# Spectral weights loaded by two DMA queues, one for each half of the partitions, the two starting at different output channels

## The chip, the cores and the metric

The kernel runs on one core of one Trainium2 chip. The metric is the device time of one execution in microseconds (us). Before the change it is 3788.58 us, the median of 3 runs (3782.95 to 3789.09).

## What is computed

The input x has 16 images of 64 channels of 128 x 128, all float32. It is normalized in 32 groups of two channels, goes through one layer, and is added to the layer's result:

```
x1 = spectral_conv2d(x, w1, w2)        # 16x16 low modes of rfft2, two blocks of rows
x2 = einsum('bchw,oc->bohw', x, conv_w) + conv_b
y  = kan_linear(kan_linear(x1 + x2, k1...), k2...)
return x + gelu(y)

def spectral_conv2d(x, w1, w2):
    x_ft = rfft2(x)
    out_ft[:, :, :16, :16]  = einsum('bixy,ioxy->boxy', x_ft[:, :, :16, :16],  w1)
    out_ft[:, :, -16:, :16] = einsum('bixy,ioxy->boxy', x_ft[:, :, -16:, :16], w2)
    return irfft2(out_ft)
```

The weights w1 and w2 are complex; each comes as a real and an imaginary tensor [input channel i, output channel o, x, y] of 64 x 64 x 16 x 16 float32. These four tensors (w1_r, w1_i, w2_r, w2_i), 4.19 MB each, are what the change is about.

## The kernel before

The program is a row of blocks. At the end of a block all engines wait for each other.

1. `forward` (lines 243 to 476) transforms the 16 images to their low modes and gathers statistics. SyncE (SP) loads each image in 8 DMAs (line 307) of 128 partitions x 8 channels x 128 values; one piece of memory that such a DMA copies is 512 bytes, and there are 1024 of them. The last thing that SP does there is `load_mix_weights(sp, t, weights[:, 2], 0, 0)` (line 343), the load of w1_r.
2. `statistics_and_mix` (lines 479 to 678) turns the statistics into one factor for each channel and image (`VectorE`, DVE, lines 615 to 664, with small matmuls at lines 547 to 558), and multiplies the modes by the weights (`mix_ps`, line 574). SP loads a small table (`pick`, line 539) and then w1_i, w2_r and w2_i (line 541).
3. `inverse_rows` (lines 681 to 785) transforms the result back along the image's height, through DRAM.
4. `second_half` (lines 788 to 1084) does the rest, tile by tile: convolution, the two spline layers, gelu. GpSimd (POOL) has its only work here, one DMA of a tile (line 906) that adds x to the result: 128 partitions x 4 KB, so 128 pieces of 4 KB.

The mix (lines 562 to 579) has two groups g: g = 0 uses w1, g = 1 uses w2. Before a group TensorE (PE) waits until both parts (real and imaginary) of its weights have landed (line 565). A group has 8 steps x; a step is 64 matmuls. A step waits for `normed` (the modes times the factors, which DVE makes at line 675) and for `mix_kept`, which says that ScalarE (ACT) has copied the result of the step but one before out of the PSUM buffer (line 595). ACT stores each copy with two DMAs on its own queue (line 600), and copies into one of two buffers only when the stores of that buffer have landed (line 594).

In SBUF the weights stand with 64 input channels on partitions 0 to 63 for one half of the rows x (8 of 16), and the same 64 input channels on partitions 64 to 127 for the other half. Each weight tensor so takes 8 DMAs of 512 KB (line 147): 4 ranges of 16 output channels, and for each both halves, one after the other. One DMA covers 64 partitions x 16 output channels x 128 values: again 1024 pieces of 512 bytes. All go through the SP queue:

```
    for o0 in range(0, C, MIX_O):
        for half in range(2):
            ...
            sp.dma_start(dst[half * C:(half + 1) * C, o0:o0 + MIX_O, :, :], ...
```

C is 64, MIX_O is 16, SH is 8.

Of the kernel before, what the change touches and what calls it, by code (L numbers as in the profile page):

```python
# [13 lines left out]
B, C, H, W = 16, 64, 128, 128  # L14
# [25 lines left out]
SH = MODES // 2  # L40
PLACES = SH + 1

MIX_O = 16
# [76 lines left out]
def first_half(nc, t):  # L120

    with ExitStack() as ctx:
        def sb(name, shape):
            return ctx.enter_context(nc.sbuf_tensor(name, shape, F32))

        modes = sb("modes", [P, PLACES, 2, 2 * MODES, B])
        stats = sb("stats", [P, B, G, 6])

        big = sb("big", [P, 4, C * W])

        rs_own = sb("rs_own", [P, 2, B])
        rs_neg = sb("rs_neg", [P, 2, B])
        mix_loaded = [[ctx.enter_context(nc.semaphore(f"mix_loaded{g}{part}")) for part in range(2)] for g in range(2)]
        t = dict(t, modes=modes, stats=stats, big=big, rs_own=rs_own, rs_neg=rs_neg, mix_loaded=mix_loaded)
        forward(nc, t)
        statistics_and_mix(nc, t)


def load_mix_weights(sp, t, dst, g, part):

    src = ((t["w1_r"], t["w1_i"]), (t["w2_r"], t["w2_i"]))[g][part]
    for o0 in range(0, C, MIX_O):
        for half in range(2):
            x0 = SH * (half if g == 0 else 1 - half)
            sp.dma_start(dst[half * C:(half + 1) * C, o0:o0 + MIX_O, :, :],
                         src[:, o0:o0 + MIX_O, x0:x0 + SH, :]).then_inc(t["mix_loaded"][g][part], 16)


def place(j):
# [91 lines left out]
def forward(nc, t):  # L243
# [8 lines left out]
    with ExitStack() as ctx:  # L252
# [8 lines left out]
        weights = big[:].rearrange("p i (o x k) -> p i o x k", x=SH, k=MODES)  # L261
# [35 lines left out]
        block = ctx.enter_context(nc.Block())  # L297

        def chunk(k):
            return slice(k * CH_GRP, (k + 1) * CH_GRP)  # L300

        @block.sync
        def _(sp):
            def load(par, b, k):
                src = t["x"][b].rearrange("c h w -> h c w") if isinstance(b, int) else \
                    t["x"][bass.ds(b, 1)].rearrange("a c h w -> h (a c) w")
                sp.dma_start(img[:, par, chunk(k), :], src[:, chunk(k), :]).then_inc(img_loaded[par][k], 16)

            sp.dma_start(dft_h_sb[:], t["dft_h"]).then_inc(tables_loaded, 16)
            load(0, 0, 0)  # L310
            sp.dma_start(eye[:], t["ident"]).then_inc(tables_loaded, 16)
            sp.dma_start(dft_w_sb[:], t["dft_w"]).then_inc(tables_loaded, 16)
            for l, (b_, s_, c_) in enumerate(((t["k1_base"], t["k1_spline"], t["k1_scaler"]),
                                              (t["k2_base"], t["k2_spline"], t["k2_scaler"]))):
                own = slice(l * C, (l + 1) * C)
                sp.dma_start(kan["spline"][own], s_).then_inc(natural_loaded, 16)
                sp.dma_start(kan["scaler"][own], c_).then_inc(natural_loaded, 16)
                sp.dma_start(kan["mats"][own, F_SILU, :], b_).then_inc(natural_loaded, 16)
                sp.dma_start(kan["mats"][own, NF, :], t["conv_w"]).then_inc(natural_loaded, 16)
            for k in range(1, N_GRP):  # L320
                load(0, 0, k)
            for k in range(N_GRP):
                load(1, 1, k)
            for d in range(2):
                sp.dma_start(t["conv_bias"][d * C:(d + 1) * C, :],
                             t["conv_b"].rearrange("(c a) -> c a", a=1)).then_inc(consts_loaded, 16)
            sp.dma_start(t["inv_w_sb"][:], t["inv_w"]).then_inc(consts_loaded, 16)
            sp.wait_ge(mats_ready, 1)
            for l in range(2):
                for d in range(2):  # L330
                    sp.dma_start(t["kan_b"][l][d * C:(d + 1) * C, :],
                                 kan["bias"][l * C:(l + 1) * C]).then_inc(consts_loaded, 16)
            with sp.Fori(1, B // 2) as b2:
                for par in range(2):
                    for k in range(N_GRP):

                        sp.wait_ge(along_h_done, 2 * N_GRP * b2 + (N_GRP * (par - 2) + k + 1))
                        sp.sem_inc(seen_by_sp, 1)
                        sp.wait_ge(stats_ready, 2 * N_GRP * b2 + (N_GRP * (par - 2) + k + 1))
                        sp.sem_inc(seen_by_sp, 1)  # L340
                        load(par, 2 * b2 + par, k)
            sp.wait_ge(consts_loaded, 112)
            load_mix_weights(sp, t, weights[:, 2], 0, 0)

        @block.vector
        def _(dve):
# [132 lines left out]
def statistics_and_mix(nc, t):  # L479
# [13 lines left out]
    with ExitStack() as ctx:  # L493
# [31 lines left out]
        mix_w = [[parts[:, 2], parts[:, 3]], [parts[:, 0], parts[:, 1]]]  # L525
# [9 lines left out]
        block = ctx.enter_context(nc.Block())  # L535

        @block.sync
        def _(sp):
            sp.dma_start(pick_sb[:], t["pick"]).then_inc(pick_loaded, 16)
            for g, part in ((0, 1), (1, 0), (1, 1)):  # L540
                load_mix_weights(sp, t, mix_w[g][part], g, part)

        @block.tensor
        def _(pe):
            pe.wait_ge(set_up, 2)
            for eo in range(2):
                ins = nc.tensor.matmul(ps_mean[:], avg[:], stats[:, :, :, 3 * eo + 1], start=(eo == 0), stop=(eo == 1))
            ins.then_inc(mean_done, 1)
            pe.wait_ge(dev_ready, 1)
            for eo in range(2):  # L550
                nc.tensor.matmul(ps_var[:], avg_sq[:], stats[:, :, :, 3 * eo + 2], start=(eo == 0), stop=False)
            for eo in range(2):
                ins = nc.tensor.matmul(ps_var[:], avg_sq[:], dev_sq[:, eo], start=False, stop=(eo == 1))
            ins.then_inc(var_done, 1)
            pe.wait_ge(rm_ready, 1)
            for i in range(2):
                rows = slice(i * C, (i + 1) * C)
                ins = nc.tensor.matmul(ps_bias[i][rows, :], conv_two[rows], pair_rm[rows, :], start=True, stop=True,
                                       tile_position=(i * C, i * C))
            ins.then_inc(bias_done, 1)  # L560

            pe.sem_inc(mix_done, 2)
            for g in range(2):
                for part in range(2):
                    pe.wait_ge(t["mix_loaded"][g][part], 32 * (C // MIX_O))
                for x in range(SH):
                    u = x % 2
                    pe.wait_ge(normed_ready, SH * g + x + 1)
                    pe.wait_ge(mix_kept, SH * g + x + 1)
                    for at in range(MIX_Q):  # L570
                        for part in range(2):
                            for col in range(2):
                                ky = col * MIX_Q + at
                                ins = nc.tensor.matmul(
                                    ps[u][col * C:(col + 1) * C, at * C:(at + 1) * C],
                                    normed[u][:, ky, 1 - part:3 - part, :, :].rearrange("p f h b -> p (f h b)"), mix_w[g][part][:, :, x, ky],
                                    start=(part == 0), stop=(part == 1), skip_group_check=True,
                                    tile_position=(0, col * C))
                    ins.then_inc(mix_done, 1)
# [534 lines left out]
```

## Time and profile before

| what | value |
|---|---|
| median of 3 runs | 3788.58 us |
| the profiled execution's own time | 3786.73 us |
| its span in the profile | 3784.9 us |
| TensorE busy | 3662.3 us (97% of the span) |
| GpSimd busy | 110.9 us (3%) |
| mix: first matmul to last store issued | 288.95 to 366.7 us of the span |

The profile was taken in one execution, and its times count from the start of the span. PE, DVE, ACT, POOL and SP are the engines; an SPq row is an instruction that SP's queue issues, and its length is the time that issuing took, not the transfer. "DMA share" is the mean busy share of the 16 DMA engines; since the packets of an engine overlap a little, it goes over 1. Lines are those of the kernel before.

### The profile page before, as it was taken

The numbers are of one execution on the slowest core, as the hardware profiler recorded it, in microseconds if no ns is written. First come the engines' busy times: TensorE is split into PE (matmuls) and PEld (weight loads), VectorE is DVE, ScalarE is ACT, GpSimd is POOL, SyncE is SP. The second block draws the span as 40 slices with busy tenths as digits, with TensorE's granted clock in tenths as the row PEclk, the third lists the DMA queues.
The fourth block names the chain that finished last, engine by engine and source line by source line (L and its number), as shares of the span: only waits on it lengthen the run. The fifth ranks groups of instructions, "written<-read, shape, count | busy, mean of one in ns | idle before, by whom it ended". The sixth has DMA issues, their size and how long they took to land.

```text
span 3784.9 us, 101254 instructions
## 1 busy us (share of the span) xinstructions
PE 3662.3 (97%) x37164; PEld 2765.6 (73%) x37164; DVE 3518.6 (93%) x3900; ACT 3391.7 (90%) x3509; POOL 110.9 (3%) x132
## 2 busy tenths in 40 slices
PE   8986599999999999999999999999999999999998
PEld 4446257777777777777777777777777777777774
DVE  7762399999999999999999999999999999999996
ACT  4531399999999999999999999999999999999996
POOL 0000000000000000000000000000000000000000
PEclk9998799999999999999999999999999999999999
DMA  9997622322322322322332332332332232232232
GB/s 263 290 248 152 232 56 60 72 66 60 72 66 60 72 67 60 72 67 60 72 69 57 72 72 55 71 72 56 70 72 57 69 72 58 68 72 58 68 72 45
DMA packets 322041, 328.62 MB, mean 87 GB/s; under 512 B 86864, under 2 KB 251216, under 8 KB 319952
## 3 DMA queue, kind: packets, MB, share of 16 engines
q1 hardware_dynamic: 301008, 256.73, 25.0%
q0 software_dynamic: 18432, 67.12, 11.2%
q10 hardware_dynamic: 2560, 4.20, 0.5%
q8 instruction: 30, 0.49, 0.1%
q14 instruction: 11, 0.09, 0.0%
HBM read 239.88 MB, written 88.08 MB: 87 GB/s over the span
## 4 chain that ended last, share of the span: by engine, by line
PE 87%; DVE 0%; issue 0%; ACT 0%; POOL 0%; POOLq 0%; ACTq 0%; DVEq 0%
PE l_ps L1057 82%; PE y_ps L1044 3%; PE y_ps L1036 2%; DVE cube2l L933 0%; DVE cube3r L933 0%; ACT above L972 0%; ACT size L983 0%; ACT offset L987 0%; ACT S L976 0%; ACT below L980 0%; DVE cube1r L933 0%; DVE cube1l L933 0%; DVE cube0l L933 0%; ACT L976 0%; DVE cube0r L933 0%
## 5 line engine op out<-in xcount | busy, mean ns | idle before, releaser
L987 ACT ACTIVATE offset<-size 128x1024 f32<-128x1024 f32 x1280 | 1240.5, 1044 | 8.1
L933 DVE SCALAR_TENSOR_TENSOR cube0r<-below,offset 128x1024 f32<-128x1024 f32 x256 | 314.3, 1228 | 57.3 <-ACT offset L987 56.7
L1057 PE MATMUL l_ps<-S,turned_w 64*64 64x512 f32 x2048 | 330.5, 592 | 8.1 <-issue 8.1
L1057 PE MATMUL l_ps<-cube1l,turned_w 64*64 64x512 f32 x2048 | 330.0, 589 | 1.0 <-issue 1.0
L1057 PE MATMUL l_ps<-cube0r,turned_w 64*64 64x512 f32 x2048 | 329.9, 591 | 0.6 <-DVE cube0r L933 0.6
L1057 PE MATMUL l_ps<-cube3r,turned_w 64*64 64x512 f32 x2048 | 329.7, 589 | 0.8 <-DVE cube3r L933 0.8
L1057 PE MATMUL l_ps<-below,turned_w 64*64 64x512 f32 x2048 | 329.9, 591 | 0.0
L1057 PE MATMUL l_ps<-cube4r,turned_w 64*64 64x512 f32 x2048 | 329.7, 589 | 0.1
L1057 PE MATMUL l_ps<-cube4l,turned_w 64*64 64x512 f32 x2048 | 329.7, 589 | 0.1
L1057 PE MATMUL l_ps<-cube3l,turned_w 64*64 64x512 f32 x2048 | 329.7, 589 | 0.1
L1057 PE MATMUL l_ps<-cube2r,turned_w 64*64 64x512 f32 x2048 | 329.6, 589 | 0.0
L1057 PE MATMUL l_ps<-cube2l,turned_w 64*64 64x512 f32 x2048 | 329.6, 589 | 0.0
L1057 PE MATMUL l_ps<-bowl,turned_w 64*64 64x512 f32 x2048 | 329.6, 589 | 0.0
L1057 PE MATMUL l_ps<-inner_cube,turned_w 64*64 64x512 f32 x2048 | 329.6, 589 | 0.0
L1057 PE MATMUL l_ps<-cube1r,turned_w 64*64 64x512 f32 x2048 | 329.2, 589 | 0.0
L1057 PE MATMUL l_ps<-cube0l,turned_w 64*64 64x512 f32 x2048 | 329.1, 590 | 0.0
L933 DVE SCALAR_TENSOR_TENSOR cube4l<-above,offset 128x1024 f32<-128x1024 f32 x256 | 314.4, 1228 | 0.0
L942 DVE SCALAR_TENSOR_TENSOR inner_cube<-below,square 128x1024 f32<-128x1024 f32 x256 | 314.4, 1228 | 0.0
L933 DVE SCALAR_TENSOR_TENSOR cube4r<-below,offset 128x1024 f32<-128x1024 f32 x256 | 314.3, 1228 | 0.0
L933 DVE SCALAR_TENSOR_TENSOR cube3l<-above,offset 128x1024 f32<-128x1024 f32 x256 | 314.2, 1227 | 0.0
L933 DVE SCALAR_TENSOR_TENSOR cube3r<-below,offset 128x1024 f32<-128x1024 f32 x256 | 314.1, 1227 | 0.0
L933 DVE SCALAR_TENSOR_TENSOR cube2l<-above,offset 128x1024 f32<-128x1024 f32 x256 | 313.9, 1226 | 0.0
(121 smaller groups left out, 7481.4 us busy)
## 6 DMA issues: line engine op xcount, KB each, us to landing
big<-in_x_dram SPq DMA_DIRECT2D x128, 512.0 KB, 7.0
x_ring<-in_x_dram SPq DMA_DIRECT2D x256, 256.0 KB, 4.0
act_out<-in_x_dram POOLq DMA_DIRECT2D x128, 512.0 KB, 6.8
out_dram<-act_out SPq DMA_DIRECT2D x128, 512.0 KB, 2.7
rows_scratch<-rows SPq DMA_DIRECT2D x16, 1024.0 KB, 7.0
rows_t<-rows_scratch SPq DMA_DIRECT2D x512, 32.0 KB, 5.5
big<-in_spec_w_r_dram SPq DMA_DIRECT2D x16, 512.0 KB, 11.1
big<-in_spec_w_i_dram SPq DMA_DIRECT2D x16, 512.0 KB, 11.2
```

What stands on the lines that cost most here:

```text
L933: nc.vector.scalar_tensor_tensor(out=cube[q][side][:], in0=distance[layer][:], scalar=EDGE - KNOTS[q], in1=offset[layer][q][:], op0=ALU.mi ...
L942: nc.vector.scalar_tensor_tensor(out=inner_cube[:], in0=below[layer][:], scalar=EDGE, in1=square[layer][:], op0=ALU.subtract, op1=ALU.mult ...
L987: nc.scalar.activation(offset[layer][q][:], size[layer][:], ACT.Square, bias=-KNOTS[q]).then_inc(offset_ready[layer], 1)
L1036: nc.tensor.matmul(y_ps[image, n * MM:(n + 1) * MM], conv_t[par][half, image], src[half, i * MM:(i + 1) * MM], start=True, stop=False, ski ...
L1044: ins = nc.tensor.matmul(y_ps[image, at:at + W], rows[half, par, h, :], inv_w_sb[half, i, :], start=False, stop=(h == HH - 1), skip_group_ ...
L1057: ins = nc.tensor.matmul(dst[cols, r * MM:(r + 1) * MM], kan_w[layer][rows_, f, :], src[rows_, n * MM:(n + 1) * MM], start=(f == 0), stop= ...
```

## The change

`load_mix_weights` gets an engine and a half as arguments, and issues the 4 DMAs of that half alone. Half 0 takes the output channels from 0, 16, 32, 48; half 1 takes them from 32, 48, 0, 16. For w1_r, still inside `forward`, SP issues half 0 and then half 1. For w1_i, w2_r and w2_i SP issues half 0 and GpSimd half 1, each from the start of the block of statistics and mix. There is one semaphore for each half, group and part, where there was one for each group and part; TensorE waits for both halves.

```
-def load_mix_weights(sp, t, dst, g, part):
+def load_mix_weights(eng, t, dst, g, part, half):
...
     src = ((t["w1_r"], t["w1_i"]), (t["w2_r"], t["w2_i"]))[g][part]
-    for o0 in range(0, C, MIX_O):
-        for half in range(2):
-            x0 = SH * (half if g == 0 else 1 - half)
-            sp.dma_start(dst[half * C:(half + 1) * C, o0:o0 + MIX_O, :, :],
-                         src[:, o0:o0 + MIX_O, x0:x0 + SH, :]).then_inc(t["mix_loaded"][g][part], 16)
+    x0 = SH * (half if g == 0 else 1 - half)
+    for n in range(0, C, MIX_O):
+        o0 = (n + half * (C // 2)) % C
+        eng.dma_start(dst[half * C:(half + 1) * C, o0:o0 + MIX_O, :, :],
+                      src[:, o0:o0 + MIX_O, x0:x0 + SH, :]).then_inc(t["mix_loaded"][half][g][part], 16)
...
             sp.wait_ge(consts_loaded, 112)
-            load_mix_weights(sp, t, weights[:, 2], 0, 0)
+            for half in range(2):
+                load_mix_weights(sp, t, weights[:, 2], 0, 0, half)
...
             for g, part in ((0, 1), (1, 0), (1, 1)):
-                load_mix_weights(sp, t, mix_w[g][part], g, part)
+                load_mix_weights(sp, t, mix_w[g][part], g, part, 0)
+
+        @block.gpsimd
+        def _(pool):
+            for g, part in ((0, 1), (1, 0), (1, 1)):
+                load_mix_weights(pool, t, mix_w[g][part], g, part, 1)
...
-                    pe.wait_ge(t["mix_loaded"][g][part], 32 * (C // MIX_O))
+                    for half in range(2):
+                        pe.wait_ge(t["mix_loaded"][half][g][part], 16 * (C // MIX_O))
```

What SP issues from the end of `forward` to the start of `inverse_rows`, before (`big` holds the weights):

```order
L147 DMA big<-in_spec_w1_r_dram 64x16x128 x8
L252 UNCONDITIONAL_BRANCH
L537 UNCONDITIONAL_BRANCH
L539 DMA pick_sb<-pick_dram 128x32
L147 DMA big<-in_spec_w1_i_dram 64x16x128 x8
L147 DMA big<-in_spec_w2_r_dram 64x16x128 x8
L147 DMA big<-in_spec_w2_i_dram 64x16x128 x8
```

The same place of SP now (the lines of the changed file are one or two higher):

```order
L148 DMA big<-in_spec_w1_r_dram 64x16x128 x8
L253 UNCONDITIONAL_BRANCH
L539 UNCONDITIONAL_BRANCH
L541 DMA pick_sb<-pick_dram 128x32
L148 DMA big<-in_spec_w1_i_dram 64x16x128 x4
L148 DMA big<-in_spec_w2_r_dram 64x16x128 x4
L148 DMA big<-in_spec_w2_i_dram 64x16x128 x4
```

SP keeps all 8 DMAs of w1_r and half of the DMAs of each of the other three tensors.

GpSimd from its start to its DMA of the second half, before:

```order
L1101 MEMSET const-uint8-127 128x1
L901 UNCONDITIONAL_BRANCH
L903 UNCONDITIONAL_BRANCH
L903 ISA
L906 REGISTER_ALU x4
L906 ISA
L906 DMA act_out<-in_x_dram 128x1024
```

And now:

```order
L1109 MEMSET const-uint8-127 128x1
L545 UNCONDITIONAL_BRANCH
L148 DMA big<-in_spec_w1_i_dram 64x16x128 x4
L148 DMA big<-in_spec_w2_r_dram 64x16x128 x4
L148 DMA big<-in_spec_w2_i_dram 64x16x128 x4
L495 UNCONDITIONAL_BRANCH
L909 UNCONDITIONAL_BRANCH
L911 UNCONDITIONAL_BRANCH
L911 ISA
L914 REGISTER_ALU x4
L914 ISA
L914 DMA act_out<-in_x_dram 128x1024
```

The twelve DMAs that SP lost stand on GpSimd, ahead of everything that it did before, and behind the end of `forward`, since the block begins there.

## Rows read from the trace of the kernel before

**Rows 1.** The page: the span in 40 slices of 94.6 us, PE, DMA

```profile
PE   8986599999999999999999999999999999999998
DMA  9997622322322322322332332332332232232232
```

**Rows 2.** Waits of PE, 259 to 370 us: total, times, longest

```profile
PE mix_ps L574 <- DMA big<-in_spec_w_i_dram: 26.2, 2, 16.0
...
PE mix_ps L574 <- ACT mixed L595: 1.6, 1, 1.6
```

**Rows 3.** Timeline of PE, 268 to 376 us: start, length, what, [idle before]

```profile
288.95 21.98 PE L574 MATMUL mix_ps<-big,stats 128*64 128x64 f32 x384 [10.13 <-DMA big<-in_spec_w_i_dram]
312.48 7.36 PE L574 MATMUL mix_ps<-big,stats 128*64 128x64 f32 x128 [1.55 <-ACT mixed L595]
335.87 28.84 PE L574 MATMUL mix_ps<-big,stats 128*64 128x64 f32 x512 [16.03 <-DMA big<-in_spec_w_i_dram]
375.25 1.23 PE L763 MATMUL rows_ps<-spec,inv_h_sb 64*128 64x512 f32 x2 [10.53 <-DMA spec<-modes_scratch]
```

**Rows 4.** Timeline 268 to 450 us: DVE's chain of statistics, its last steps

```profile
268.02 0.68 DVE L629 TENSOR_TENSOR picked<-mean_bg,pick_sb 128x512 f32<-128x512 f32 x1
...
274.41 0.69 DVE L629 TENSOR_TENSOR picked<-ps_var,pick_sb 128x512 f32<-128x512 f32 x1 [4.98 <-PE ps_var L553]
...
280.75 0.69 DVE L675 TENSOR_TENSOR stats<-modes,rs_neg 128x512 f32<-128x512 f32 x1 [0.35 <-DVE modes L664]
281.36 1.29 DVE L675 TENSOR_TENSOR stats<-modes,rs_own 128x512 f32<-128x512 f32 x2
```

**Rows 5.** Timeline of ACT, 288 to 376 us

```profile
302.54 0.60 ACT L595 ACTIVATE mixed<-mix_ps 128x512 f32<-128x512 f32 x1 [5.57 <-DMA modes_scratch<-mixed]
...
321.09 0.60 ACT L595 ACTIVATE mixed<-mix_ps 128x512 f32<-128x512 f32 x1 [5.73 <-DMA modes_scratch<-mixed]
...
324.94 0.60 ACT L595 ACTIVATE mixed<-mix_ps 128x512 f32<-128x512 f32 x1 [3.25 <-DMA modes_scratch<-mixed]
```

**Rows 6.** Stretches: length, PE, PEld, DVE, ACT, POOL busy, PEclk, DMA share, GB/s

```profile
60.00:230.00 170.00, 170.00 (x1523) 82.14 (x1520) 132.59 (x391) 88.65 (x183) 0.00 (x0) 1.00 1.16 290
263.00:288.00 25.00, 7.46 (x14) 2.53 (x12) 13.71 (x33) 0.22 (x1) 0.00 (x0) 0.57 1.22 194
300.00:321.00 21.00, 18.21 (x320) 17.50 (x315) 10.46 (x17) 2.39 (x4) 0.00 (x0) 1.00 1.17 233
342.00:362.00 20.00, 20.00 (x364) 20.00 (x361) 9.48 (x15) 3.60 (x6) 0.00 (x0) 1.00 0.36 78
```

**Rows 7.** DMAs of w1_r issued 247 to 258 us

```profile
L147 SPq DMA_DIRECT2D big<-in_spec_w_r_dram x5: 2502/2622/3114, 245.3 to 255.8; - x5
...
DMA to landing us min/median/max: 11.0/11.2/11.4
```

**Rows 8.** Timeline of the SP queue, 226 to 262 us (issuing only)

```profile
239.25 19.67 SPq L147 DMA_DIRECT2D big<-in_spec_w_r_dram  x8
259.56 1.99 SPq L539 DMA_DIRECT2D pick_sb<-pick_dram  x1
261.60 0.60 SPq L147 DMA_DIRECT2D big<-in_spec_w_i_dram  x1
```

**Rows 9.** ACT's stores issued 288 to 300 us, beside the weights

```profile
L600 ACTq DMA_DIRECT2D modes_scratch<-mixed x4: 489/494/595, 293.7 to 297.9; - x4
...
DMA to landing us min/median/max: 7.1/7.4/8.1
```

**Rows 10.** ACT's stores issued 335 to 362 us, with no weights in flight

```profile
L600 ACTq DMA_DIRECT2D modes_scratch<-mixed x12: 481/487/502, 340.6 to 359.1; - x12
...
DMA to landing us min/median/max: 2.3/2.3/2.3
```

**Rows 11.** GpSimd's DMA of line 906: ns min/median/max, and to landing

```profile
L906 POOL DMA_DIRECT2D act_out<-in_x_dram x128: 862/862/1007, 510.2 to 3776.4; - x128
...
DMA to landing us min/median/max: 5.4/6.8/7.7
```

More of the change, by code:

```diff
@@ L132, in first_half @@
         rs_neg = sb("rs_neg", [P, 2, B])
-        mix_loaded = [[ctx.enter_context(nc.semaphore(f"mix_loaded{g}{part}")) for part in range(2)] for g in range(2)]
+        mix_loaded = [[[ctx.enter_context(nc.semaphore(f"mix_loaded{half}{g}{part}")) for part in range(2)]
+                       for g in range(2)] for half in range(2)]
         t = dict(t, modes=modes, stats=stats, big=big, rs_own=rs_own, rs_neg=rs_neg, mix_loaded=mix_loaded)
```

## The prediction

> **What bounds the kernel now.** I read the page's slices first. TensorE is busy nine tenths or more of every slice from the sixth on but the last [rows 1], so nothing that happens before about 470 us is hidden later: whatever the start of the program saves is saved in full, and no more. The change touches 239 to 370 us only. There the view of the waits names what PE waits for: 26.2 us for the imaginary weights, in two waits, and 1.6 us for ACT's copy [rows 2]. The timeline of PE places them. The first group of the mix starts at 288.95, 10.13 us idle before it; the second starts at 335.87 with 16.03 us idle before it, and runs without a break for 28.84 us [rows 3]. What follows (stores, rows, second half) hangs on the end of that group. So the question is when w1_i and when w2_i land, and what is late next.
>
> What could come next, if the weights came at once? For the first group it is DVE's chain: its first `normed` tile is done at 281.36 + 1.29 = 282.7 [rows 4], so PE could start near 283.3, 5.7 us earlier. For the second group it is ACT. PE finished the first group at 312.48 + 7.36 = 319.84 [rows 3], but the first step of the second group reuses the PSUM buffer of the seventh step, which ACT copied at 321.09 to 321.69, and the second step that of the eighth, copied by 325.54 [rows 5]. PE could start at 321.7, 14.2 us earlier, and then run at 28.84 / 8 = 3.6 us a step.
>
> **Why the weights are slow.** The stretches show it. While images are loaded, the 16 DMA engines are full (share 1.16) and move 290 GB/s; while weights are loaded they are as full (1.22) and move 194 GB/s [rows 6]. Both transfers consist of 1024 pieces of 512 bytes, so piece size is not the reason. They differ in that an image goes to 128 partitions and a weight DMA to 64, and in the addresses in DRAM. SP has about four weight DMAs in flight (11.2 us to landing, one issued each 2.6 us [rows 7]), of both halves in turn, and that does not help: in one queue every engine meets the halves in the same order. The Trainium skill, "SBUF — State Buffer", section "Door 1: The DMA port swizzle", says that partitions 0 to 63 reach 8 of 16 ports and 64 to 127 the other 8. By that rule, the 194 is a limit of 8 ports, and the trace agrees as far as 194 against 290 goes.
>
> **The change, part by part.**
>
> *Bytes.* A tensor is 8 x 512 KB = 4.19 MB; a half is 2.10 MB. Three tensors, 12.58 MB, are now split 6.29 MB to SP and 6.29 MB to GpSimd. w1_r stays with SP; its last DMA lands at 255.8 + 11.2 = 267.0 [rows 7], so at 263, where GpSimd's first can flow, (267 - 263) x 194 = 0.78 MB of w1_r is left. The order of w1_r's halves I cost at nothing: one queue either way.
>
> *The rate with two queues.* No row shows two queues that fill different halves. Bounds: 194 GB/s (no gain) and 290 GB/s (as good as 128 partitions) [rows 6]. Two engines that share the way into a half collide when both are at the same half, and don't when one is at each; with queues taken in turn and no fixed phase, I take the middle, 245. I assume equal shares for the two queues.
>
> *Before the first group.* 263 to 271: SP works off w1_r at 97 GB/s (0.78 / 97 = 8 us), GpSimd brings 0.78 MB of w1_i; both are on the second half, hence 194 in total. From 271: SP's half of w1_i, 2.10 MB at 122 GB/s, takes 17.2 us, to 288.2. That is the old 288.95: **nothing gained in the first group**, because the rate that goes up is shared with weights not yet needed. At 290 GB/s it is 14.5 us, to 285.5 (3.4 us gained); at 194, 21.6 us, to 292.6 (3.7 us lost, which has room before the second group's weights). The `pick` table stands behind w1_r in SP's queue and lands some 4 us later than now; DVE used it at 268.02, and has idled 4.98 us by 274.41 [rows 4], which hides that.
>
> *Before the second group.* At 288, 11.8 - 17 x 0.245 = 7.6 MB are left. With ACT's stores beside them the total rises to 233 GB/s [rows 6], of which a step's 256 KB in 4.64 us (302.54 to 321.09, four steps [rows 5]) is 56, so the weights had 177, some 20 less than alone. I take 245 - 20 = 225: 34 us, to 322. At 290 - 20 it is 25.5 us from 288, to 313.4, before ACT is ready; at 194 it is about 336, as now, which also closes the sum against the trace. So the second group starts at 322 instead of 335.87: **-14**.
>
> *What the stores lose.* Beside the weights they took 7.4 us to land [rows 9], without them 2.3 [rows 10]. That sets ACT's pace in the first group. A third queue can push it to some 8.2, over three pairs of steps 2.4 us; between 0 and 5, I take **+2**. The second group then runs free of weights as before, 3.6 us a step.
>
> *GpSimd's issuing.* It starts with SP's first w1_i, at 261.6 [rows 8]. Its known DMA is issued in 0.862 us, for 128 pieces [rows 11]; the new ones have 1024. If the cost is per instruction: 12 x 0.86 = 10 us, no limit. If per piece: 8 x 0.862 = 6.9 us each, 83 us in all. I take something like 2 to 4 us (part of the 0.86 must be fixed), hidden: 12 of them have to be done by 322 - 3 = 319, so up to 57 / 12 = 4.8 us each costs nothing. The Trainium skill, "DMA: Bandwidth & Descriptors", section "Anatomy of one DMA", says that many descriptors can be emitted before their added cost shows; by that rule this term is 0, and no row here shows it. What follows on GpSimd is the DMA at 510 us [rows 11], far off. The extra semaphore waits of PE are 4 and end at once.
>
> *Sum:* -14 + 2 = **-12 us**. The profiled execution took 3786.73; 3786.7 - 12 = 3774.7. The median of the runs is 1.9 us above that execution, so I forecast **3776.5 us**.
>
> **The rivals.**
>
> *The queues go on sharing one limit (the change doesn't do what it says).* If 194 comes from the addresses in DRAM, or if the same 16 engines are the limit whichever queue feeds them, the weights land at 335.9 again, and the time is 3788. The different DRAM addresses of the two transfers speak for it, and that alternating halves did nothing; 290 GB/s for the same pieces speaks against. Chance 0.20, within 0.2%. The Trainium skill, "SBUF — State Buffer", section "Can I just issue two DMAs to hit both halves?", speaks for this rival and against the change: two transfers to the two halves at once came out only 6% faster than one, since they serialize. By that figure my estimate would be 3785; no row here shows two such queues.
>
> *GpSimd's issuing becomes the bound.* Place: the twelve DMAs from 261.6 on; price 6.9 us each by the row's pieces. The last is issued at 261.6 + 83 = 344.6, lands some 3 us later, and the second group starts near 347.5 instead of 335.9: +11.7, **3800**. It costs time from (335.9 - 261.6 - 3) / 12 = 5.9 us a DMA, and shows over 0.2% (7.6 us, about what a measurement can tell from no change) from 6.6. For it: nothing in the row separates fixed from per piece. Against: pure proportion would leave nothing for the instruction. Chance 0.13; between 4.8 and 6.6 us, where the result stays within 0.2% for most of it, 0.08.
>
> *Unequal shares.* If one queue takes nearly all, the other's half of w1_i waits for all three tensors' halves on the first, 6.3 MB at 194: the first group starts near 310, ends about 339, and the second near 370 instead of 364.7: +5, **3793**. ACT's stores and SP's loads did share in the stretch at 233 GB/s, which speaks against. Chance 0.03.
>
> *Better than forecast.* 290 GB/s and the first group at 283.3: -5.7 - 14.2 = -20, **3768**. It is within the forecast's own chance of 0.56, which spans -8 to -20.
>
> **How the numbers follow.** Forecast (-8 to -20) 0.56; shared limit 0.20; slow issuing 0.13 and its middle 0.08; shares 0.03. Faster by over 0.2%: 0.56 plus the quicker part of the middle, 0.58. Slower by over 0.2%: 0.13. Within: the rest, 0.29. The range 3767 to 3792 takes in the best case and no change with the spread of the runs, and leaves out the slow issuing's far end.
>
> **What would show it.** In the trace after: between 272 and 288 the GB/s of all DMAs should read 230 to 290, not 194; the first group starting at 285 to 290; the second at 320 to 326, its idle time before it under 4 us and put down to ACT as much as to a DMA; GpSimd's DMA instructions of line 148 under 4.8 us each; PE from the second group on shifted as a block. I am wrong if GB/s stays near 200 (no port gain), if GpSimd's rows are 6 us or more, or if ACT's stores take over 10 us to land and stretch the first group.

## The result: 3794.78 us, slower by 0.2%, and the profile after

The changed kernel takes 3794.78 us (median of 16 runs, 3792.04 to 3796.03) against 3787.02 us before (16 runs on the same chips, 3782.01 to 3789.37). The ratio is 1.0019, with a 95% interval of 1.0012 to 1.0026: 7.8 us lost where I had forecast 12 gained, and above the end of my range. The profiled execution has a span of 3793.8 us.

The timeline of PE in the changed kernel (start, length, what, idle before it), to be held against [rows 3]:

```profile
310.62 21.86 PE L582 MATMUL mix_ps<-big,stats 128*64 128x64 f32 x384 [30.51 <-DMA big<-in_spec_w_i_dram]
334.84 36.00 PE L582 MATMUL mix_ps<-big,stats 128*64 128x64 f32 x640 [2.36 <-ACT mixed L603]
381.08 10.13 PE L771 MATMUL rows_ps<-spec,inv_h_sb 64*128 64x512 f32 x32 [10.24 <-DMA spec<-modes_scratch]
```

The first group starts at 310.62, 21.7 us later than before; PE idled 30.5 us for w1_i. The second group follows without any wait for weights: the row at 334.84 holds the last two steps of the first group and all eight of the second (640 = 10 x 64 matmuls). The mix ends at 370.84, where it ended at 335.87 + 28.84 = 364.71 before: 6.1 us later. All the weights of the second group were there in time; those of the first were not. (DVE's chain, the next thing that the first group needs, was done with its first tile at 282.66 + 1.28 = 283.94.)

What the queues did, first GpSimd's, then SP's (issuing only):

```profile
261.04 3.49 POOL L148 DMA_DIRECT2D big<-in_spec_w_i_dram  x4 [260.45 <-POOLq L253]
264.49 3.29 POOL L148 DMA_DIRECT2D big<-in_spec_w_r_dram  x4
267.72 3.31 POOL L148 DMA_DIRECT2D big<-in_spec_w_i_dram  x4
```

```profile
260.48 2.27 SPq L541 DMA_DIRECT2D pick_sb<-pick_dram  x1
262.79 35.15 SPq L148 DMA_DIRECT2D big<-in_spec_w_i_dram  x4
297.98 15.20 SPq L148 DMA_DIRECT2D big<-in_spec_w_r_dram  x4
313.23 11.49 SPq L148 DMA_DIRECT2D big<-in_spec_w_i_dram  x4
```

GpSimd had issued all twelve of its DMAs by 271, at 0.84 us each, no more than for its DMA of 128 pieces [rows 11]. SP needed 35 us to issue four. The groups of line 148 give durations and times to landing, for GpSimd alone:

```profile
L148 POOL DMA_DIRECT2D big<-in_spec_w_i_dram x8: 842/876/1007, 261.0 to 270.1; - x8
...
DMA to landing us min/median/max: 10.9/21.6/32.9
```

GpSimd's last DMA landed at 270.1 + 32.9 = 303, so that queue moved its 6.29 MB between about 267 and 303, some 175 GB/s. Three stretches of the changed kernel (length, busy times, PEclk, DMA share, GB/s; the first and last with SP's loads into one half alone):

```profile
250.00:259.00 9.00, 7.24 (x155) 5.54 (x153) 2.50 (x6) 2.06 (x5) 0.00 (x0) 1.00 1.22 182
282.00:300.00 18.00, 0.00 (x0) 0.00 (x0) 3.70 (x6) 0.00 (x0) 0.00 (x0) 0.50 1.06 208
302.00:310.00 8.00, 0.00 (x0) 0.00 (x0) 0.00 (x0) 0.00 (x0) 0.00 (x0) 0.50 1.22 182
```

The two queues together reach 208 GB/s, of which some 30 are left for SP. From 302 to 310 only SP's queue is still at work, at 182 GB/s, and brings the rest of w1_i. Why the shares are so unequal shows in the page's list of queues (packets, MB, share), here before the change:

```profile
q1 hardware_dynamic: 301008, 256.73, 25.0%
q0 software_dynamic: 18432, 67.12, 11.2%
```

and after it:

```profile
q1 hardware_dynamic: 288528, 250.44, 24.1%
q0 software_dynamic: 20160, 73.41, 12.0%
```

q1 is SP's queue, q0 GpSimd's. Twelve DMAs left q1 with 12480 packets, 1040 each: 1024 of 512 bytes and 16 small ones. On q0 the same twelve came to 1728 packets, 144 each: 128 of 4096 bytes and 16 small ones. GpSimd's queue joins eight pieces of 512 bytes into one packet. If an engine takes one packet of each queue in turn, GpSimd gets eight ninths: 185 of 208 GB/s, SP 23. The trace keeps every packet with its queue, start and size, and they can be counted: from 280 to 300 us 1005 packets of q0 began and 1021 of q1, and they carried 183 and 26 GB/s. So the two queues took turns nearly one for one, and the bytes followed the size of a packet. A preference for GpSimd's queue, the obvious other reading, would show in more packets for it, and does not.

### The profile page after: what moved, and what is told of

Read it like the earlier page. It is cut to its first block, busy times and chain, and to the rows that moved or that the text cites. A ratio compares the mean times of both kernels' runs of the same rounds, so it can differ in the third digit from the quotient of the medians.

```text
span 3793.8 us, 101256 instructions
## 1 busy us (share of the span) xinstructions
PE 3665.4 (97%) x37164; PEld 2305.9 (61%) x37164; DVE 3519.0 (93%) x3900; ACT 3391.7 (89%) x3509; POOL 122.0 (3%) x144
## 4 chain that ended last, share of the span: by engine, by line
PE 87%; DVE 0%; issue 0%; ACT 0%; POOL 0%; POOLq 0%; ACTq 0%; DVEq 0%
PE l_ps L1065 81%; PE y_ps L1044 3%; PE y_ps L1052 3%; DVE cube2l L941 0%; DVE cube3r L941 0%; ACT above L980 0%; ACT size L991 0%; ACT offset L995 0%; ACT S L984 0%; ACT below L988 0%; DVE cube1r L941 0%; DVE cube1l L941 0%; DVE cube0l L941 0%; ACT L984 0%; DVE cube0r L941 0%
## 5 line engine op out<-in xcount | busy, mean ns | idle before, releaser
L941 DVE SCALAR_TENSOR_TENSOR cube1l<-above,offset 128x1024 f32<-128x1024 f32 x256 | 312.1, 1219 | 0.0
L941 DVE SCALAR_TENSOR_TENSOR cube0l<-above,offset 128x1024 f32<-128x1024 f32 x256 | 312.1, 1219 | 0.0
L941 DVE SCALAR_TENSOR_TENSOR cube2r<-below,offset 128x1024 f32<-128x1024 f32 x256 | 312.1, 1219 | 0.0
L941 DVE SCALAR_TENSOR_TENSOR cube1r<-below,offset 128x1024 f32<-128x1024 f32 x256 | 312.1, 1219 | 0.0
L1065 PE MATMUL l_ps<-S,turned_w 64*64 64x512 f32 x2048 | 298.6, 592 | 7.8 <-issue 7.8
L1065 PE MATMUL l_ps<-cube3r,turned_w 64*64 64x512 f32 x2048 | 298.3, 589 | 0.9 <-DVE cube3r L941 0.9
L1065 PE MATMUL l_ps<-cube3l,turned_w 64*64 64x512 f32 x2048 | 298.3, 589 | 0.1
L1065 PE MATMUL l_ps<-cube4r,turned_w 64*64 64x512 f32 x2048 | 298.3, 589 | 0.1
L1065 PE MATMUL l_ps<-cube4l,turned_w 64*64 64x512 f32 x2048 | 298.3, 589 | 0.1
L1065 PE MATMUL l_ps<-cube0r,turned_w 64*64 64x512 f32 x2048 | 297.9, 590 | 0.6 <-DVE cube0r L941 0.6
```

What stands on the lines that cost most here:

```text
L941: nc.vector.scalar_tensor_tensor(out=cube[q][side][:], in0=distance[layer][:], scalar=EDGE - KNOTS[q], in1=offset[layer][q][:], op0=ALU.mi ...
L1065: ins = nc.tensor.matmul(dst[cols, r * MM:(r + 1) * MM], kan_w[layer][rows_, f, :], src[rows_, n * MM:(n + 1) * MM], start=(f == 0), stop= ...
```

## The experiments

The counts say how the queues shared. That this sharing is what made the kernel slower is for the runs to show. **Theory A**: the queues share by packets, so GpSimd's queue takes eight ninths and brings w2, which nobody needs yet, while SP's half of w1_i waits. **Theory B**: work on GpSimd's queue beside SP slows both. Beside these stood my forecast's other premise, that two queues on different halves can pass the limit of one.

### GpSimd holds w2 back

```
             for g, part in ((0, 1), (1, 0), (1, 1)):
+                if g == 1 and part == 0:
+                    pool.wait_ge(t["mix_loaded"][0][0][1], 16 * (C // MIX_O))
                 load_mix_weights(pool, t, mix_w[g][part], g, part, 1)
```

> GpSimd issues its four DMAs of w1_i, then waits until SP's half of w1_i has landed, and only then issues its eight of w2. Theory A (the changed kernel is slow because GpSimd's queue moves 4096 bytes at each turn against SP's 512, so it takes 184 of 208 GB/s and brings w2 while SP's half of w1_i waits): GpSimd's w1_i is in by 276, SP then has the engines alone, 2.6 MB at 194 GB/s, and the first group starts at 288 to 291 instead of 310.6; w2 then takes 8.39 MB at about 200 GB/s, the second group starts at 329 to 334, and the time is 3781 to 3786, 2 to 6 us under before. Theory B (any work on GpSimd's queue beside SP slows both, whatever is asked for first): the first group starts after 300 and the time stays at 3790 or more.

Measured: 3786.82 us (ratio to before 1.0002, interval 0.9992 to 1.0012). The PE timeline:

```profile
291.73 11.42 PE L584 MATMUL mix_ps<-big,stats 128*64 128x64 f32 x200 [10.87 <-DMA big<-in_spec_w_i_dram]
...
334.31 28.88 PE L584 MATMUL mix_ps<-big,stats 128*64 128x64 f32 x512 [7.11 <-issue]
```

The first group comes 18.9 us earlier than in the changed kernel, by one wait that reorders the loads, and the whole loss is gone. Theory A stands, B falls. Both starts and the time lie just past the late edge of what I expected (291, 334 and 3786). Once w2 flows, the packets are again one for one: from 298 to 320 us 1079 of GpSimd's queue and 1056 of SP's. Nothing is gained over before either.

### ACT's queue in place of GpSimd's, for w1_i

```
-            for g, part in ((0, 1), (1, 0), (1, 1)):
-                load_mix_weights(pool, t, mix_w[g][part], g, part, 1)
...
         def _(act):
+            load_mix_weights(act, t, mix_w[0][1], 0, 1, 1)
```

ACT issues these DMAs ahead of its square root. SP loads all of w2, half 0 then half 1 of each tensor.

> The second half of w1_i goes through ACT's queue instead of GpSimd's, all of w2 through SP alone; both queues then move pieces of 512 bytes. Theory A: shares are equal, so from 272 to 284 both queues move alike. If two queues on different halves can pass the 194 GB/s of one (my forecast's assumption), the stretch reads 240 to 290 GB/s and the first group starts at 284 to 286; if the limit is one for both queues, it reads 190 to 210 and the first group starts at 288 to 290, as before. Time 3783 to 3789 either way, since w2 goes by SP alone. Theory B: first group later than 295.

Measured: 3787.41 us (1.0001, 0.9992 to 1.0011); the first group at 287.24, the second at 336.24. Two stretches of it:

```profile
265.00:270.00 5.00, 0.78 (x2) 0.23 (x2) 4.03 (x4) 0.00 (x0) 0.00 (x0) 0.50 1.22 178
276.00:283.00 7.00, 0.40 (x5) 0.29 (x4) 5.21 (x22) 0.22 (x1) 0.00 (x0) 0.66 1.17 287
```

From 276 to 283 SP fills half 0 and ACT half 1, both by packets of 512 bytes: 287 GB/s, the rate of an image load [rows 6]. From 265 to 270 only half 1 was being filled, by SP (the rest of w1_r, up to 268) and ACT (w1_i), and it was 178, from 266 to 267 too, when both queues moved about equal amounts. So two queues on different halves do pass the limit of one, and fully, when their turns are equal. It lasted for one tensor only, and the first group came 1.2 us later than I expected for this outcome (284 to 286).

### Both halves from the same output channels

```
-        o0 = (n + half * (C // 2)) % C
+        o0 = n
```

> The change without its shift of output channels: both halves start at channel 0. Theory A: the same picture as the changed kernel, first group at 310 to 312, 205 to 210 GB/s from 280 to 300. Rival (the shift costs or gives DRAM bandwidth): the stretch reads more than 5 GB/s off, and the first group moves by over 2 us.

Measured, in a single run: 3795.03 us, the first group at 310.95, 208 to 210 GB/s from 280 to 300. The shift of the channels does nothing here. With equal turns, where both halves are really filled at once, leaving it out was not tried.

### One GpSimd DMA in flight

```
+        if alone:
+            eng.wait_ge(t["mix_loaded"][half][g][part], 16 * (n // MIX_O + 1))
...
-                load_mix_weights(pool, t, mix_w[g][part], g, part, 1)
+                load_mix_weights(pool, t, mix_w[g][part], g, part, 1, alone=True)
```

> The change with GpSimd waiting for each of its DMAs to land before it issues the next. Theory A: its queue is empty for some 2 us of every 5, in which SP has 194 GB/s; SP's mean goes from 25 to about 90 GB/s, and the first group starts at 291 to 298 instead of 310.6; the second at 329 to 337. Time 3783 to 3792. Theory B: GpSimd's queue costs whenever it runs, and total GB/s from 280 to 300 falls below 190 with the first group after 300.

Measured: 3814.16 us (1.0071, 1.0055 to 1.0088), the first group at 305.99, the second at 360.24. A clear miss of the size. The timeline of GpSimd says why:

```profile
272.18 0.85 POOL L148 DMA_DIRECT2D big<-in_spec_w_i_dram  x1 [9.99 <-DMA big<-in_spec_w_i_dram]
283.55 0.82 POOL L148 DMA_DIRECT2D big<-in_spec_w_i_dram  x1 [10.52 <-DMA big<-in_spec_w_i_dram]
...
342.32 0.82 POOL L148 DMA_DIRECT2D big<-in_spec_w_i_dram  x1 [5.28 <-DMA big<-in_spec_w_i_dram]
```

Beside SP's full queue a DMA that starts on an empty queue lands 11 us after its issue; once SP has nothing left, 5.7. I had allowed for the transfer and 2 us. So both groups now wait for GpSimd's own DMAs: its fourth of w1_i, issued at 294.70, lands at 305.8 and the first group starts at 305.99; its last, issued at 354.11, lands at 359.9 and the second group starts at 360.24. The total of 184 to 188 GB/s from 280 to 300 and the first group after 300 are the numbers that I had given to theory B, so by these this run does not part the theories. The packets speak for A: from 288 to 293 us SP's queue moved 91 GB/s (theory A had 90), against 26 in the changed kernel.

### All of w1_i and w2 by GpSimd

```
-                load_mix_weights(sp, t, mix_w[g][part], g, part, 0)
...
-                load_mix_weights(pool, t, mix_w[g][part], g, part, 1)
+                load_both(pool, t, mix_w[g][part], g, part)
```

`load_both` is the old function: both halves in turn, by one queue.

> All DMAs of w1_i and w2 by GpSimd alone, the halves in turn; SP keeps w1_r. Theory A (208 GB/s is what GpSimd's large turns reach on one half at a time, and SP beside it adds nothing): 200 to 210 GB/s from 280 to 300 with one queue; w1_i is in at 263 + (0.8 + 4.2 MB) / 0.2 = 288 to 291, first group at 288 to 292, all in at 331 to 335, second group 331 to 336, time about that of before, 3782 to 3789. Rival (the two halves did help in the changed kernel): GB/s falls to 190 or less.

Measured, in a single run: 3784.28 us; first group at 290.99, second at 331.97; a stretch of it:

```profile
282.00:288.00 6.00, 0.00 (x0) 0.00 (x0) 3.35 (x6) 0.00 (x0) 0.00 (x0) 0.50 1.04 197
```

As expected. GpSimd's queue alone has 197 to 203 GB/s; in the changed kernel SP's ninth beside it made 208. So the second queue on the other half gave the changed kernel nearly nothing. The packets fit that: from 280 to 300 the engines were busy with GpSimd's packets, all for half 1, for 0.90 of the time, and with SP's for 0.17.

### w1_r with the halves in turn

```
-            for half in range(2):
-                load_mix_weights(sp, t, weights[:, 2], 0, 0, half)
+            load_both(sp, t, weights[:, 2], 0, 0)
```

> The change, with the eight DMAs of w1_r in the order of before (halves in turn). Theory A: 193 instead of 182 GB/s from 250 to 259, the block of statistics starts 0.9 us earlier (259.6), w1_r is in some 1.5 us earlier, the first group starts at 309 to 310 instead of 310.6; time 3792 to 3795. Rival (the order does nothing): 182 GB/s and 260.5 again.

Measured, in a single run: 3794.95 us; 194 GB/s from 250 to 255, `pick` issued at 259.86 instead of 260.48, first group at 309.45. So the order of w1_r's halves, which I had costed at nothing, costs some 1.2 us at the first group. The packets were one for one here too, 923 of GpSimd's queue and 922 of SP's from 280 to 298.

### w1 by two hardware queues, w2 by SP

```
-            for half in range(2):
-                load_mix_weights(sp, t, weights[:, 2], 0, 0, half)
+            load_mix_weights(sp, t, weights[:, 2], 0, 0, 0)
+            load_mix_weights(sp, t, weights[:, 3], 0, 1, 0)
...
+            act.wait_ge(consts_loaded, 112)
+            load_mix_weights(act, t, weights[:, 2], 0, 0, 1)
...
         def _(act):
+            load_mix_weights(act, t, mix_w[0][1], 0, 1, 1)
```

The first two parts are in `forward`, ACT's behind its last image; the last part is at the start of the next block. SP loads w2 there, the halves in turn.

> w1 goes by SP (half 0, all eight DMAs inside forward) and ACT (half 1: w1_r behind its last image, w1_i at the start of the next block), w2 by SP alone with the halves in turn as before; GpSimd loads nothing. Theory A (two queues that move equal pieces into different halves reach 290 GB/s): the stretch from 262 to 280 reads 280 to 290 GB/s, the first group starts at 284 to 290, all weights are in by 317 to 323, the second group starts at 318 to 324 instead of 335.9, time 3771 to 3777. Theory C (the 287 GB/s seen beside ACT's queue held for a short overlap only): the stretch falls back under 230 and the second group starts after 330, time 3783 or more.

Measured: 3782.84 us (0.9989, 0.9979 to 0.9999): faster than before by 4.3 us, where I had expected 10 to 16. The timeline of ACT:

```profile
254.75 11.88 ACTq L148 DMA_DIRECT2D big<-in_spec_w_r_dram  x4
267.31 18.52 ACTq L148 DMA_DIRECT2D big<-in_spec_w_i_dram  x4
285.86 1.28 ACT L599 ACT_TABLE_LOAD   x1 [30.86 <-issue]
```

Issuing blocked ACT for 11.9 us inside `forward`, so the next block began at 267.3 instead of 259.6, and then again for 18.5 us ahead of the square root. The first group started at 301.00, the second at 332.49, with its weights there and ACT's copy awaited last. The rate reached 253 GB/s from 265 to 270 and fell back to 202 to 222 from 270 to 300. These are the numbers that I had given to theory C, that the high rate holds for a short overlap only. The other reading is that SP's w2 went to both halves in turn and met ACT on half 1; this run alone does not decide it, the one with equal turns below does.

### The same, with GpSimd for the last part

Half 1 of w2_i by GpSimd, once half 1 of w1 has landed; SP keeps half 0 of it.

> As the run before, but the second half of w2_i comes by GpSimd, which waits until the second half of w1 has landed. Theory A: GpSimd's 4096-byte turns take 180 GB/s for some 12 us, which costs nothing now since nothing urgent waits; total some 205 instead of 177 beside the stores; second group within 3 us of the run before, in either direction, time 3769 to 3778.

Measured: 3787.24 us (0.9999, 0.9989 to 1.0009). In its trace the first group starts at 298.61 and the mix ends at 361.99, 0.7 us later than in the run before, as expected. The time is a miss: I had expected 3769 to 3778. The two profiled executions differ by 1.0 us (3785.51 and 3784.54), as their traces do; that the medians differ by 4.4, the traces do not explain.

### Equal turns, each queue on its own half

```
+            load_both(sp, t, weights[:, 2], 0, 0)
...
+            load_mix_weights(sp, t, mix_w[0][1], 0, 1, 0)
+            load_mix_weights(sp, t, mix_w[1][0], 1, 0, 0)
+            load_both(sp, t, mix_w[1][1], 1, 1)
...
         def _(act):
+            load_mix_weights(act, t, mix_w[0][1], 0, 1, 1)
             act.wait_ge(var_ready, 1)
             nc.scalar.activation(root[:], var[:], ACT.Sqrt).then_inc(root_ready, 1)
+            load_mix_weights(act, t, mix_w[1][0], 1, 0, 1)
```

GpSimd loads nothing.

> w1_r by SP with the halves in turn, as before. In the next block SP loads half 0 of w1_i and of w2_r, ACT half 1 of w1_i and, right behind its square root, half 1 of w2_r; w2_i goes by SP with the halves in turn. GpSimd loads nothing. Theory A (two queues with equal pieces, each on its own half, reach some 290 GB/s): 280 to 290 GB/s from 276 to 290; first group at 285 to 288; ACT's first stores stand behind its last weights, which delays one copy by some 3 us; all weights in by 322 to 328, the second group starts there instead of at 335.9; time 3775 to 3780. Rival (issuing on ACT's queue holds its copies up longer than the weights gain): first copy after 296 and the second group after 332, time 3783 or more.

Measured: 3777.41 us (11 runs, 3773.95 to 3780.14; ratio to before 0.9979, 0.9970 to 0.9988). It beats both kernels. PE, then a stretch of it:

```profile
286.74 21.70 PE L586 MATMUL mix_ps<-big,stats 128*64 128x64 f32 x384 [7.56 <-ACTq L600]
...
324.14 28.87 PE L586 MATMUL mix_ps<-big,stats 128*64 128x64 f32 x512 [7.57 <-DMA big<-in_spec_w_i_dram]
```

```profile
276.00:288.00 12.00, 1.54 (x26) 1.48 (x28) 7.30 (x26) 0.21 (x1) 0.00 (x0) 0.67 1.17 288
```

288 GB/s for twelve microseconds and 277 from 290 to 300, so theory C falls. In the stretch shown SP's queue began 3461 packets and ACT's 3398, and they moved 145 and 143 GB/s. The second group starts 11.7 us before the old 335.87.

### The same without ACT's half of w2_r

> The run before without ACT's half of w2_r: ACT loads only half 1 of w1_i, and SP loads w2 alone with the halves in turn. Theory A: first group at 285 to 288, w2 in 1 to 4 us earlier than before (332 to 335), time 3783 to 3786. The difference to the run before is what a second equal queue gives for one tensor more: 6 to 9 us.

SP loads all of w2, the halves in turn. Measured: 3783.42 us (0.9990, 0.9981 to 0.9999), first group at 288.32, second at 333.96. The second equal queue for one tensor more is worth 9.8 us at the second group and 6.0 us of the median. The profiled executions differ by 9.8 us too (3787.08 and 3777.33); that of this run was the longest of its ten.

## Why the prediction was wrong

*What bounds the kernel*: right. The time of every profiled execution moved with the end of the mix in it: what came behind that end took between 3422 and 3425 us in all versions. Of the 8.9 us between the profiled executions before and after (7.8 between the medians), 370.84 - 364.71 = 6.1 arose up to the end of the mix. Most of the rest arose behind it, in the rows transform: from its first matmul to the second half's first it took 448.50 - 375.25 = 73.3 us before and 457.10 - 381.08 = 76.0 after. No instruction differs there. The first 32 matmuls took 8.87 us before and 10.13 after. In the six microseconds from the first of them the granted clock was 0.69 before and 0.50 after, the lower of its two levels:

```profile
375.25 8.87 PE L763 MATMUL rows_ps<-spec,inv_h_sb 64*128 64x512 f32 x32 [10.53 <-DMA spec<-modes_scratch]
375.00:381.00 6.00, 5.75 (x20) 2.57 (x22) 2.32 (x4) 2.08 (x4) 0.00 (x0) 0.69 0.15 35
381.00:387.00 6.00, 5.92 (x14) 2.56 (x16) 1.75 (x3) 1.60 (x3) 0.00 (x0) 0.50 0.15 40
```

The first row is of before's timeline; the other two are stretches (PEclk is the third number from the end), the first of before, the second of after. Other versions lie between (73.9 with w1 by two hardware queues, 75.6 with equal turns). Whether that is chance or follows from where PE stands, I did not settle.

*The rate with two queues, bounds 194 and 290, taken 245*: two queues on different halves can pass the limit of one, and the upper bound is what they give, 287 and 288 GB/s in two runs, where the two queues have equal packets. For the pair of queues in this change it measured 208. I had not asked how much each turn of a queue moves. My sign "GB/s stays near 200 (no port gain)" came true, but the reason in its brackets is not the cause.

*"I assume equal shares for the two queues"*: this is the step that failed, and it carried both terms behind it. The shares were 183 to 26 GB/s, 7 to 1, by packets of 8 to 1 in size. With them, "nothing gained in the first group" (288.2) became 310.62, and the -14 at the second group became +6 at its end. My rival of unequal shares had the first group near 310, the mix's end near 370 and the time at 3793: measured 310.62, 370.84 and 3794.78. I had given it 0.03, because ACT's stores and SP's loads shared at 233 GB/s [rows 6]. That pair has packets of 2 KB against 512 bytes on two hardware queues, and says nothing on how GpSimd's queue packs. Nor did the page of before: GpSimd's 18432 packets for 67.12 MB are of 4 KB, but so are the pieces of its only DMA there. It showed that packets of 4 KB exist beside those of 512 bytes, which was reason enough to ask; that this queue joins small pieces, only the changed kernel's page shows. That the rival came out to 1 or 2 us in all three numbers is in part luck: it let one queue take everything, at 194 GB/s, where it took seven eighths of 208.

*The stores' loss, +2*: ACT's stores beside SP took 7.4 us in the changed kernel too, as before [rows 9]; 0 instead of +2, since GpSimd had finished by then.

*GpSimd's issuing*: hidden, as forecast, and at the cheap bound instead of the 2 to 4 us each that I had taken: 12 x 0.84 = 10.1 us. The rule of the Trainium skill, "DMA: Bandwidth & Descriptors", section "Anatomy of one DMA", that many descriptors can be emitted before their added cost shows, agrees with the trace: 1024 pieces take no longer to issue than 128. But both left as 128 packets of 4 KB, and no run here shows GpSimd issuing a DMA of more.

*The shared limit as a rival, 0.2*: not the cause of the loss. The section "Can I just issue two DMAs to hit both halves?" of the Trainium skill's "SBUF — State Buffer" has 6% for two transfers at once over a single one. This change shows 14% over one half alone (208 against 182) and 7% over one queue with the halves in turn (194); two hardware queues with equal pieces show 61% and 48% (287 against 178 and 194). Where the page says that two such transfers serialize, these runs decide otherwise.

*The order of w1_r's halves, 0*: mis-sized by some 1.2 us. One half at a time is 182 GB/s, both in turn 194. So alternating the halves in one queue did help a little, where the forecast says that it does nothing. *The `pick` table*, 4 us later: right in kind. It was used at 273.82 instead of 268.02, and DVE's chain ended 1.3 us later, hidden by the wait for weights; 0.9 of the 1.3 came with the later start of the block.

## What to carry to other kernels

When work is split over two DMA queues, read in the page how many bytes a packet of each has (MB over packets, less the 16 small ones of each DMA), for the very DMAs that are split: in these runs the queues took turns by packets, and packets of 4096 bytes left a queue with packets of 512 bytes an eighth to a ninth of the rate. Put on the greedy queue only what is needed first, or hold back by a wait what is needed later. To fill 64-partition tiles at full rate, give each half its own queue with equal pieces, keep them on different halves all the time, and see that issuing does not block an engine that has something else to do.

## What the runs showed of the hardware that I had not expected

- GpSimd's queue joins pieces of 512 bytes, eight at a time, into packets of 4096; SP's and ACT's queues send each piece as a packet (144 against 1040 packets for the same DMA).
- Two full queues take turns nearly packet for packet: 1005 to 1021 in 20 us of the changed kernel, 1079 to 1056 in 22 us with GpSimd holding w2 back, 923 to 922 in 18 us with w1_r in turn, 3461 to 3398 in 12 us with equal turns on two hardware queues.
- Two hardware queues that load 512-byte pieces into different halves reach 287 to 288 GB/s; on one half 176 to 182; one queue with the halves in turn 194.
- A DMA on an empty queue lands about 5 us later when another queue is full: GpSimd's 512 KB landed after 11 us beside SP and 5.7 us alone, ACT's stores after 7.4 and 2.3 us [rows 9, 10]. How much of this is waiting and how much the shared rate is not shown.
- Where GpSimd loads all of w1_i and w2, it issued 15 DMAs of 1024 pieces one behind the other and the next only at 288.4, 14.5 us later:

```profile
268.15 5.76 POOL L157 DMA_DIRECT2D big<-in_spec_w_r_dram  x7
288.40 0.83 POOL L157 DMA_DIRECT2D big<-in_spec_w_r_dram  x1 [14.49 <-issue]
```
